# Macaron block on one core: one 1 MB accumulating transfer for each pair of products in place of two, a first and a last chunk worked in token halves, and new tables of order

## The reference

```python
x = x + 0.5 * ffn(layernorm(x))      # ffn 1
x = x + ssm(layernorm(x))            # selective scan
x = x + 0.5 * ffn(layernorm(x))      # ffn 2, the same weights

def ffn(x):                          # hidden width 1408; w quantised to -1, 0, 1
    hidden = sigmoid(x @ q(w1).T) * (x @ q(w2).T)
    return hidden @ q(w3).T

def ssm(x):                          # 16 states per channel
    xz = x @ W_x.T                   # 128 columns dt_raw, 16 columns b, 16 columns c
    dt = softplus(dt_raw @ W_dt.T + b_dt)
    for t in range(T):
        h = exp(dt[t] * a) * h + dt[t] * b[t] * x[t]     # h is 512 x 16
        y[t] = sum over the 16 states of h * c[t]
    return y + x * D_param
```

## Time and profile before

| | |
|---|---|
| median of 3 runs | 840.51 us (837.66, 843.51, 840.51) |
| the profiled execution | 838.59 us, span 836.7 us |
| busy PE / DVE / ACT / POOL | 651.4 / 674.6 / 554.6 / 658.4 us |
| head, up to the first scan | 96.5 us |
| a middle chunk | 88.4 us |
| PE clock granted, mean | 0.894 of full |

### The profile page before, as it was taken

One profiled execution on the slowest core, in us unless ns is written; L12 is line 12 of the kernel. 1 busy time (PEld: TensorE's weight loads), 2 busy tenths in 40 slices (PEclk: granted clock), 3 DMA queues, 4 the chain that ended last, 5 costly groups with the idle time before them and its releaser, 6 DMA issues.

```text
span 836.7 us, 13876 instructions
## 1 busy us (share of the span) xinstructions
PE 651.4 (78%) x4920; PEld 538.5 (64%) x4920; DVE 674.6 (81%) x1079; ACT 554.6 (66%) x1157; POOL 658.4 (79%) x516
## 2 busy tenths in 40 slices
PE   4688587368889888989899888988898876147578
PEld 4576375257677776777578767876687755136367
DVE  4962798699978997899978997899789978799721
ACT  5752764967696678776885679566966795366231
POOL 0261597799899989999899989998999898689112
PEclk7798797679999999999999998999999999569779
DMA  9400378677774978297829784878659673957300
GB/s 362 133 1 1 104 168 180 156 148 163 177 169 108 208 179 187 48 231 167 189 51 227 166 179 111 182 171 173 157 126 202 151 179 82 235 122 141 76 1 26
DMA packets 42694, 122.12 MB, mean 146 GB/s; under 512 B 5888, under 2 KB 14848, under 8 KB 42624
## 3 DMA queue, kind: packets, MB, share of 16 engines
q0 software_dynamic: 19152, 69.74, 44.5%
q1 hardware_dynamic: 23472, 51.49, 18.0%
HBM read 47.03 MB, written 4.46 MB: 62 GB/s over the span
## 4 chain that ended last, share of the span: by engine, by line
POOL 27%; DVE 20%; ACT 17%; PE 15%; issue 14%; DMA 7%; DVEq 0%; POOLq 0%; ACTq 0%
DVE states L881 11%; POOL shared L1078 11%; PE work L392 10%; DMA shared<-shared 7%; POOL hid_lo L1064 6%; PE stat L392 4%; DVE shared L893 3%; POOL shared L1090 3%; ACT decay L700 3%; POOL shared L1089 2%; POOL x_lo L1058 2%; POOL shared L282 1%; ACT tanh L643 1%; ACT hid_hi L651 1%; POOL square L286 1%
## 5 line engine op out<-in xcount | busy, mean ns | idle before, releaser
L1078 POOL TENSOR_TENSOR shared<-shared,b_row 128x1024 f32<-128x1024 f32 x128 | 331.2, 2658 | 39.8 <-DVE shared L282 21.8
L392 PE MATMUL work<-x_hi,q 128*128 128x256 f16 x1408 | 325.8, 281 | 45.8 <-DVE hid L856 25.8
L392 PE MATMUL work<-x_lo,q 128*128 128x256 f16 x1408 | 324.8, 280 | 0.0
L881 DVE TENSOR_TENSOR_SCAN states<-decay,last_state,shared 128x256 f32<-128x256 f32 x448 | 301.7, 738 | 4.9 <-DVE shared L893 0.5
L700 ACT ACTIVATE decay<-shared,a_neg 128x256 f32<-128x256 f32 x512 | 221.9, 468 | 95.6 <-DVE states L881 93.5
L1064 POOL TENSOR_TENSOR hid_lo<-hid,hid_hi 128x256 f16<-128x256 f32 x176 | 144.5, 1102 | 58.0 <-ACT hid_hi L651 57.9
L392 PEld LDWEIGHTS work<-x_hi,q 128*128 128x128 f16 x1408 | 142.5, 101 | 71.6 <-DVE hid L856 30.0
L392 PE MATMUL work<-hid_hi,q 128*128 128x256 f16 x704 | 165.9, 282 | 5.2 <-POOL hid_lo L1064 3.6
L392 PE MATMUL work<-hid_lo,q 128*128 128x256 f16 x704 | 165.9, 282 | 0.0
L893 DVE TENSOR_TENSOR shared<-states,c_row 128x1024 f32<-128x1024 f32 x128 | 156.0, 1219 | 9.5 <-DMA shared<-shared 2.2
L392 PEld LDWEIGHTS work<-x_lo,q 128*128 128x128 f16 x1408 | 141.7, 101 | 22.0 <-issue 1.1
(11 more groups left out here) (99 smaller groups left out, 733.1 us busy)
## 6 DMA issues: line engine op xcount, KB each, us to landing
shared<-shared POOLq DMA_DIRECT2D x133, 512.0 KB, 6.6
b_row<-bc_dram SPq DMA_DIRECT2D x32, 512.0 KB, 4.9
c_row<-bc_dram SPq DMA_DIRECT2D x32, 512.0 KB, 5.2
x_in<-xT SPq DMA_DIRECT2D x8, 512.0 KB, 5.4
outT<-shared SPq DMA_DIRECT2D x7, 512.0 KB, 4.5
shared<-w1T SPq DMA_DIRECT2D x4, 704.0 KB, 6.9
shared<-w2T SPq DMA_DIRECT2D x4, 704.0 KB, 11.8
shared<-w3T SPq DMA_DIRECT2D x3, 768.0 KB, 13.4
```

Of the source, the lines that this page charges most:

```text
L392: return nc.tensor.matmul(out, lhsT, rhs, start=start, stop=stop)
L881: nc.vector.tensor_tensor_scan(out=states[:, k, :], data0=decay[pair][:, k % 2, :], data1=dbx[:, g % DBX_RING, k, :], initial=state, op0=A ...
L1078: nc.gpsimd.tensor_tensor(dbx[:, g % DBX_RING, :, :], u[:, par, :, :], bcast(b_row[:, group % 2, n % ROWS, :]), ALU.mult).then_inc(dbx_don ...
```

## The change

1. **Transfers.** `prod` keeps its four slots (PROD_RING = 4). `homes(c)` is a strided view of the two slots of `sums`, that of x2(c) and that of y(c), and one transfer of 1 MB adds two neighbouring products to both. There is one semaphore count of 16 for each pair. DVE's `times_c` waits once per pair, at the even product.
2. **Tables.** They are new throughout, and `at` looks first for an entry for chunk 0 (`_first`) or chunk 7 (`_last`). ACT's reads of z and the four pieces of `softplus_logs` have places of their own.
3. **Head.** Layernorm 1 of chunk 0 is worked in two halves of 128 tokens. The projection of b and c comes ahead of that of dt_raw, the first up product of chunk 1 behind both. Softplus of chunk 0 is worked in two pairs of channel tiles, and so is POOL's first product.
4. **Tail.** The order of the last sums changes, PE takes the mean from two parts, layernorm 2 is worked in token halves, and the four down tiles have banks, residuals and stores of their own. ACT runs one idle Tanh early.

```diff
-DBX_RING, PAIR_RING, X_RING, Y_RING = 3, 2, 3, 2
+DBX_RING, PROD_RING, X_RING, Y_RING = 3, 4, 3, 2
...
+def at(table, c, name):
+    own = name + ("_first" if c == 0 else "_last" if c == NC - 1 else "")
+    return table[own] if own in table else table[name]
...
-            return 32 * (PAIRS * (c // 2) + n)
+        def homes(c):
+
+            even, odd = c % X_RING, X_RING + c % Y_RING
+            return sums[:, even:odd + 1:odd - even, :, :]
+
+        def added(c, n):
+
+            return pairs_added[c % 2], 16 * (NS // 2 * (c // 2) + n // 2 + 1)
...
-                if g // 2 >= PAIR_RING:
-                    before = g // 2 - PAIR_RING
-                    dve.wait_ge(pair_added[before // PAIRS % 2], pairs_added(before // PAIRS, before % PAIRS + 1))
+                if g >= PROD_RING and n % 2 == 0:
+                    dve.wait_ge(*added((g - PROD_RING) // NS, (g - PROD_RING) % NS))
...
-                nc.gpsimd.dma_start(x2(c), prod_of(c, 2 * pair), accum_op=ALU.add).then_inc(pair_added[c % 2], 16)
-                nc.gpsimd.dma_start(y(c), prod_of(c, 2 * pair + 1), accum_op=ALU.add).then_inc(pair_added[c % 2], 16)
+                    pool.wait_ge(*added(c, n - 2))
+                pool.wait_ge(prod_done, NS * c + n + 2)
+                nc.gpsimd.dma_start(homes(c), prod_pair(c, n), accum_op=ALU.add).then_inc(added(c, n)[0], 16)
...
+            def half_var_of(i, n, j):
+                pe.wait_ge(half_square, n + j + 1)
+                for k in range(KD):
+                    ins = mm(decay[j][:, 1, 0:1], square[i][:, k, token_half(j)], mean_w[:, 0:1], k == 0, k == KD - 1)
+                ins.then_inc(half_var, 1)
...
-            ffn_up(1, 0, 0)
             pe.wait_ge(params_loaded, 16 * 6)
+            pe.wait_ge(half_out, 2)
+            for k in range(KD):
+                ins = mm(states[0:BC, 0, :], wbc[:, k, :], xln[:, k, :], k == 0, k == KD - 1)
+            ins.then_inc(bc_mm, 1)
             project_dt_raw(0)
             project_dt(0, 0, decay[0])
             project_dt(0, 1, decay[1])
-            project_bc(0, stat)
-            for h in range(1, UP_EARLY):
+            pe.wait_ge(ln_hi[0], 2)
+            pe.wait_ge(ln_lo[0], 2)
+            for h in range(UP_EARLY):
                 ffn_up(1, 0, h)
...
+            def first_dt_and_u(pair, n):
+                two = slice(2 * pair, 2 * pair + 2)
+                dve.wait_ge(first_ln, pair + 1)
+                dve.wait_ge(first_tail, 2 * pair + 1)
+                nc.vector.tensor_tensor(sp_t[:, two, :], sp_l[:, two, :], sp_t[:, two, :], ALU.add).then_inc(first_tail, 1)
+                dve.wait_ge(first_tail, 2 * pair + 2)
+                dve.wait_ge(z_read, 2 * pair + 2)
+                nc.vector.tensor_tensor(dt[:, 0, two, :], dt[:, 0, two, :], sp_t[:, two, :], ALU.add).then_inc(first_dt, 1)
+                dve.wait_ge(first_dt, pair + 1)
+                nc.vector.tensor_tensor(u[:, 0, two, :], dt[:, 0, two, :], xln[:, two, :], ALU.mult).then_inc(first_u, 1)
...
             for h in range(KH):
-                ffn_up(ffn2_pass(NC - 1), 1, h)
+                ffn_up(f, 1, h)
+            pe.wait_ge(hid_done, KH * f + KH)
...
+                    for part in (hid_hi, hid_lo):
+                        ins = mm(LAST_BANKS[m][:, 0, :], q3[:, h, m * P:(m + 1) * P], part[:, h, :], n == 0, n == 2 * KH - 1)
+                        n += 1
+                ins.then_inc(last_down, 1)
```

More of the change, by code:

```diff
@@ L65, in due, with ffn1_due @@
 def due(times, now):
     return [n for n, t in enumerate(times) if t == now]
+def ffn1_due(table, c, name, now):
+    return [(b, h) for b in (c + 1, c + 2) if b < NC for h in due(at(table, b - 1, name), now - 10 * NS * (b - 1 - c))]
 def macaron(nc, xT, w_xT, w_dtT, b_dt, a_log, d_param, w1T, w2T, w3T, outT):
@@ L148, in macaron @@
         gamma_bank = decay[0]
[L149 removed]
+        LAST_BANKS = [work[2], work[0], work[1], decay[0]]
         w_loaded = [[sem(f"w{m}_{q}_loaded") for q in range(KD)] for m in range(3)]
@@ L760, in _ @@
-            read_bc(0)
-            softplus_logs(0)
+            for pair in range(2):
+                two = slice(2 * pair, 2 * pair + 2)
+                act.wait_ge(z_done, pair + 1)
+                for m in range(2 * pair, 2 * pair + 2):
+                    nc.scalar.activation(sp_e[:, m, :], decay[pair][:, m % 2, :], ACT.Abs, bias=bdt[:, m:m + 1]).then_inc(first_abs, 1)
+                act.wait_ge(first_abs, 2 * pair + 2)
+                nc.scalar.activation(sp_e[:, two, :], sp_e[:, two, :], ACT.Exp, scale=-1.0).then_inc(first_exp, 1)
@@ L1047, in _ @@
             for h in range(KH):
                 hidden(ffn2_pass(NC - 1), 1, h)
-            for pair in range(2):
-                residual(ffn2_pass(NC - 1), 1, pair, x2_out, x2_out)
+            for m in range(KD):
+                dve.wait_ge(last_down, m + 1)
+                nc.vector.scalar_tensor_tensor(out=x2_out[:, m, :], in0=LAST_BANKS[m][:, 0, :], scalar=0.5 / HID_SCALE,
+                                               in1=total[:, m, :], op0=ALU.mult, op1=ALU.add).then_inc(last_res, 1)
```

500 lines of the change are left out of this document (296 added, 204 removed).

## The result

The changed kernel takes 852.95 us (median of 4 runs, 849.38 to 860.92) where the kernel before, run beside it, takes 839.09 (836.74 to 843.51): ratio 1.018, interval 1.0131 to 1.0228. It is slower; I had forecast 820.5. The profiled execution spans 851.2 us against 836.7, 14.5 more.

A forecast was written before the change was run, and what follows sets the result against it. Middle chunks were taken as bound by DVE, then ACT, then PE, with POOL second. Head 5.5, chunk 0 2.8, tables 7.2, chunk 7 3.0 and tail 1.5 sum to 20.0 us off 838.59; predicted median 820.5, range 800 to 835.

The forecast's parts named there:

- What bounds the kernel: Middle chunk: some 59 us of saturated DVE, 18 of ACT, 11.3 of PE's down product; POOL nearly full but second.
- Transfers: Pair transfers: issue 1.4 us, POOL relieved 2.9 us a chunk (bounds 0 and 7.0), landing 8.0 to 8.9, path gain 0.
- Tables: Chunks 1 to 6: moved hidden products and ffn1's centring save 1.2 us a chunk, 7.2 for six; bounds nothing and 3.9 a chunk.
- My own caution: Steady tables of before may fit the machine better than two moved gates suggest, since only those edits were followed.
- Head: Before the first scans: halves, reordered projections and paired softplus start step 1 about 5.5 us earlier than 100.68; bounds 3 and 8.
- the prediction's sign for "cost more than it overlapped": Head: a first scan after 94 us would mean DVE's half-wide softplus list cost more than it overlapped.
- Chunk 0: Chunk 0: 4.5 us of waits taken back, 1.7 lost at chunk 1's first gate (bound 4), net 2.8.
- Chunk 7: Last chunk: add of y issued one step earlier takes back 3.0 us of DVE's 3.99 wait; bounds 0 and 4.
- Tail: After the last scan: halves save about 2 us, mean 0.3, down's later start costs 0.8; net 1.5, bounds -1 and 4.
- The one on the slow side: Rival: each pair waits on POOL for one slow landing past 10.5 us, giving about 873 us; chance 0.05.
- Its sign: Sign of the slow rival: a DVE wait of over 1 us on the DMA in most pairs.
- POOL was the bound: Rival: POOL's relief counts, 4.7 us a chunk in place of 1.2, giving 799.5 us; chance 0.17.

The follow-up runs named there:

- e4: Changed kernel with two 512 KB transfers per pair and the steady tables (chunks 1 to 6) of before: ratio 0.9975 to the kernel before.
- e3: Changed kernel, one transfer per pair kept, with the steady tables (chunks 1 to 6) of before: ratio 1.0100 to the kernel before.
- e2: Kernel before with only one point changed, each pair sent as one 1 MB transfer to both homes: ratio 1.0117 to the kernel before.
- e1: Changed kernel with each pair issued as two 512 KB transfers again, new tables kept: ratio 1.0117 to the kernel before.
- e16: Changed kernel with a third buffer for y so that the two homes are adjacent in all chunks: ratio 0.9974 to the kernel before.
- e15: Changed kernel with old steady tables, one transfer, and a third y buffer making the homes adjacent in all chunks: ratio 0.9949 to the kernel before.
- e9: Changed kernel with two transfers, old steady tables, six product buffers, y added after the sixth pair, last four products singly onto x: ratio 1.0079.

## Why the prediction was wrong

**What bounds the kernel:** half right. POOL did not bind: 34 us less of it bought nothing. But I wrote that DVE runs nearly gapless outside 415 to 443, and read that as slack for the DMA. In chunks 2 to 6 of before DVE waits 0.3 to 1.0 us at the second layer norm's centring, which stands at the end of the chain from the last pair over y. So small a wait is no cover: it means that there is next to no slack; I should have followed it back to the landing.

**The sizes.** I forecast 20 us less and 15 more came (1.8%). In runs, the change is e4, then e3 over e4, then the changed kernel over e3. All but the transfer and the steady tables (e4) gave 2 us, where head, chunks 0 and 7 and tail stood at 12.8; the one transfer cost 10.5 where I had 0; the tables cost 6.6 where I had 7.2 gained.

**Transfers, the step that failed:** "By rows 5 nothing directly, so I cost it at 0 on the path", and behind it "8.0 to 8.9 costs 0 to 0.5 a pair only where nothing else runs". DVE's products did wait for landings, 16.7 us in all. The issue I took as 1.4 measured 1.20, relief 8 x (1.76 - 1.20) = 4.5 a chunk, within the bounds. As a middle value the landing was right too: 7.9 us at the shortest, a median of 8.7. The spread was what I left out: the longest took 13.2, before 11.0 from a pair's first issue. I priced a ring and a chain by the middle landing, and it is the long ones that are waited for. With the tables as they were, this term was +10 us (e2: 1.0117 of 839), not 0. The Trainium skill, "DMA: Bandwidth & Descriptors", The descriptor swizzle, counts one piece per partition for a contiguous 1 MB. The trace agrees: with adjacent homes a transfer has 128 pieces fewer (7,040 over the 55 that were scattered), and the case hung on that. I used it to price POOL's time and not the landing.

**Tables, 7.2 us gained:** the second step that failed; with two transfers they cost 1.4% (e1 over e4), and the two moved hidden products became part of a row of four waits, 4.4 us in chunk 4 against 3.3 there before. The wait that I meant to fill did go: for the centring of ffn 1 DVE waited 6.9 us in chunks 1 to 5 before and 0.8 now, but the waits for tanh grew from 22.4 to 35.2 in chunks 1 to 6. With adjacent homes the new steady tables cost 0.25% (e16 over e15, intervals overlapping), their waits for the centring gone (0.9 against 7.9) and those for tanh up (35.5 against 27.2). My own caution, that I followed two edits only, was the right one.

**Head, 5.5:** step 1 came 0.3 us later in the profiled execution. The normalised chunk was ready at 76.4 us, where I had 74.5 and before had 78.6. Then PE's timeline:

```profile
76.56 3.57 PE L435 MATMUL states<-xln,wbc 128*32 128x256 f32 x8 [0.87 <-DVE xln L982]
80.06 1.99 PE L435 MATMUL stat<-xln,wx 128*128 128x256 f32 x8
```

The product of B and C, 1.86 us in the earlier trace rows, lasted 3.57: from 73.1 to 80.0 us the granted clock was at its 1.2 GHz level. Before, the up product stood in that stretch and took the slow clock. So ACT read the raw dt at 82.09 us, where before did at 82.08. I had taken a duration at 2.4 GHz into a stretch at 1.2. This execution is a late one: the same order of the head stands in sixteen experiments, and step 1 begins at 99.7 to 100.0 us in twelve of them and at 101.0 to 102.0 in four, where the head of before has 100.68 and, in e2, 101.52. So the term was about 1 us, not 5.5 and not nothing. Then DVE's second list ran from 90.71 to 95.46 with the first pair's scan behind it, as the prediction's sign for "cost more than it overlapped" said.

**Chunk 0, net 2.8:** from step 1 to chunk 1 it gained 0.8; chunk 1 lost 4.4, where I had 1.7 and 4 as the bound, and not one of its waits on DVE is for the DMA. With two transfers and the old steady tables (e4) it lost 2.0. **Chunk 7, 3.0:** the mean's wait fell from 3.99 to 0.62 as forecast, and DVE's DMA waits rose from 1.9 to 4.7 us; net 0.7. e9's 71.2 shows that 4 us can be had in this chunk, though by another edit.

**Tail, 1.5:** from centring to the first up product 10.0 became 7.9, as forecast. But from the last scan to that centring 10.3 became 14.1 (DVE's and PE's timelines, the last row that of before):

```profile
798.92 1.23 DVE L1167 TENSOR_TENSOR shared<-shared 128x1024 f32<-128x1024 f32 x1 [2.23 <-DMA shared<-shared]
...
801.46 6.45 PE L435 MATMUL stat<-shared,mean_w 128*128 128x256 f32 x16 [5.50 <-DVE shared L1169]
...
808.01 1.28 DVE L972 TENSOR_TENSOR centred<-xln,stat 128x512 f32<-128x512 f32 x2 [4.15 <-PE stat L435]
```

```profile
790.25 1.22 PE L392 MATMUL stat<-square,mean_w 128*128 128x256 f32 x2 [6.63 <-DVE square L288]
```

Half of it, 1.9 us, is the late landing: the first of the last sums starts 5.0 us behind the last scan, before 3.1. The other half is the mean, for which I had 0.3 gained: it is sixteen products on PE, 6.45 us, where before two products, 1.22 us together, stood behind a fold on DVE of 1.1. Both ran at the 1.2 GHz level (granted 0.5 from 800.2 to 807.0 now, from 786.3 to 806.8 before), so the clock isn't the difference. With two transfers the new tail is 52.1 us (e4), 3.4 under before.

**The rivals.** The one on the slow side came true in part: late landings, but not at every pair. Its sign, a DVE wait of over 1 us in most pairs, was met at seven of 63. I gave it 0.05 because I asked that eight landings of 10.5 us fill the chunk. In chunk 4 of the changed kernel three landings of eight were over 10 us (11.04, 10.06, 11.01), and DVE waited after the first, since POOL, the ring and the centring each wait for single pairs, not for the sum. How many are late doesn't settle it either: e16's chunk 4 has two over 10 us (10.84, 10.38) and lasts 88.5. "POOL was the bound" would have given 799.5: excluded, e16 has POOL at 75.2 of 88.5 and is no faster per chunk than before.

**Open:** why 256 pieces of 4 KB in one instruction land 0.8 us later, at the shortest, than the same pieces in two (7.9 against 7.1 from the first issue), and whether it is the number of pieces or the gap between the two homes, which changed together; how the loss divides between ring, POOL's order and chain, which were not separable; and the tables' cost with two transfers.

## What to carry to other kernels

Before two transfers are merged, lay their destinations side by side: scattered, this merge cost 1.2%, and side by side it cost nothing. Look for a gain in the number of pieces, not of instructions, and don't count on it: here it was 0.2%, within the intervals. Merging also moves the first count to the end of all bytes, so follow every wait that ended on a landing, however short, back to its issue and ask what is still moving then. A table of places is one schedule: judge it whole, and price a product that is moved by the clock of the stretch that it moves into.

## What was not expected of the hardware

A POOL issue of an accumulate costs 0.87 us for 128 pieces, be they 4 KB (512 KB) or 8 KB (1 MB), and 1.20 for 256 pieces of 4 KB. At the shortest, 512 KB lands 4.6 us after its issue, 1 MB in 8 KB pieces 7.0, in 4 KB pieces 7.9. One 4 KB piece takes an engine 342 ns and one 8 KB piece 635 (medians), so that the accumulate queue's share fell only from 44.5% to 41.9% of the sixteen engines' span. The Trainium skill, "DMA: Bandwidth & Descriptors", Anatomy of one DMA, fits one DMA as 2.0 us plus its bytes at 436 bytes per ns. The trace doesn't agree for these accumulates: from 512 KB to 1 MB they add 2.4 us, half that rate, so the measured rate is to be used for them.
